# Weights loaded in pieces, blanks set by ScalarE and VectorE, smaller chunks of row maxima, and a new step order in a two-layer cross-attention and mixture-of-experts kernel

## What is computed

```python
x = x + attn0(layernorm(x), ctx, ctx)      # 16 heads of 8; 77 keys; softmax; Wo
x = x + moe0(layernorm(x))                 # 8 experts (128 -> 256 -> 128, relu squared), top 2 of 8
x = x + attn1(ctx, layernorm(x))           # 16 heads, 77 keys; relu guards; its own layernorm, gamma
x = x + block2(layernorm(x))
# block2: self-attention over 512 keys, rotary q and k, low-rank k and v;
#         r1 = rmsnorm(src + attention); shared SwiGLU + 8 routed experts (top 2 in one group);
#         rmsnorm(r1 + shared + routed)
```

## Time and profile before

| | us |
|---|---|
| median of 3 runs (range) | 365.19 (364.46 to 366.49) |
| profiled execution, its own time | 366.7 |
| its span in the trace | 364.9 |
| TensorE busy | 314.7 (86%) |
| VectorE busy | 267.6 (73%) |
| ScalarE busy | 158.9 (44%) |
| GpSimd busy | 51.4 (14%) |
| TensorE clock granted, mean | 0.944 |

### The profile page before, as it was taken

The page is one execution under the profiler, slowest core; times in us unless marked ns, Lnnn a source line. Parts: engine busy times, 40 slices in busy tenths (PEclk is TensorE's granted clock), DMA queues, the critical chain, the costliest instruction groups (busy, mean ns, idle before and its releaser), DMA issues.

```text
span 364.9 us, 5099 instructions
## 1 busy us (share of the span) xinstructions
PE 314.7 (86%) x1880; PEld 139.6 (38%) x1880; DVE 267.6 (73%) x693; ACT 158.9 (44%) x180; POOL 51.4 (14%) x40
## 2 busy tenths in 40 slices
...
GB/s 203 270 289 56 14 25 2 56 1 2 1 2 115 5 12 0 89 0 55 133 0 2 7 1 2 100 81 2 195 2 0 9 1 2 0 0 2 30 0 29
DMA packets 13448, 16.35 MB, mean 45 GB/s; under 512 B 3568, under 2 KB 12016, under 8 KB 13040
## 3 DMA queue, kind: packets, MB, share of 16 engines
...
...
## 4 chain that ended last, share of the span: by engine, by line
PE 42%; DVE 26%; issue 17%; DMA 5%; POOL 4%; ACT 3%; SPq 1%; POOLq 0%; DVEq 0%; ACTq 0%
PE pairs_ps L557 28%; DVE mx L1044 7%; PE out_ps L557 6%; PE misc_ps L557 4%; DVE mx L1048 3%; DMA qT<-qpl 3%; DMA qT<-mpl 3%; POOL pT L520 3%; DVE ACC L1214 2%; ACT pT L851 2%; DVE turned L932 1%; DVE XN L960 1%; POOL rstd L492 1%; DVE rest L932 1%; DVE ACC L932 1%
## 5 line engine op out<-in xcount | busy, mean ns | idle before, releaser
L851 ACT ACTIVATE pT<-pairs_ps 128x1024 f32<-128x1024 f32 (+1 forms) x96 | 94.4, 1022 | 84.3 <-PE pairs_ps L557 83.5
L1044 DVE TENSOR_REDUCE mx<-pairs_ps 128x2 f32<-128x1024 f32 x64 | 74.3, 1216 | 0.6 <-PE pairs_ps L557 0.3
L557 PE MATMUL pairs_ps<-experts,hid 128*128 128x128 f32 (+1 forms) x352 | 62.2, 334 | 0.1
L492 POOL TENSOR_TENSOR rstd<-var,consts 128x4 f32<-128x4 f32 x14 | 14.6, 1044 | 263.9 <-DVE var L952 134.9
L557 PEld LDWEIGHTS pairs_ps<-experts,hid 128*128 128x128 f32 x352 | 44.9, 192 | 16.0 <-issue 16.0
L557 PE MATMUL misc_ps<-ones,zeros 128*128 128x512 bf16 x138 | 43.2, 427 | 3.2 <-POOL ones L544 2.5
L557 PE MATMUL pairs_ps<-XT,experts 128*128 128x512 f32 x96 | 45.3, 614 | 0.6 <-DVE mx L1048 0.5
L557 PE MATMUL out_ps<-pT,V 128*32 128x512 f32 x256 | 33.3, 603 | 0.0
L1048 DVE TENSOR_REDUCE mx<-pairs_ps 128x8 f32<-128x616 f32 x32 | 23.7, 793 | 12.3 <-PE pairs_ps L557 12.3
L520 POOL TENSOR_SCALAR pT<-pT 77x1024 f32<-77x1024 f32 x8 | 24.9, 3126 | 38.0 <-ACT pT L851 38.0
L1214 DVE SCALAR_TENSOR_TENSOR X<-pairs_ps,gw,X 128x128 f32<-128x128 f32 x64 | 18.0, 344 | 16.0 <-PE pairs_ps L557 15.8
...
## 6 DMA issues: line engine op xcount, KB each, us to landing
qT<-qpl SPq DMA_DIRECT2D x36, 128.0 KB, 2.5
...
kT<-kpl SPq DMA_DIRECT2D x12, 128.0 KB, 2.5
...
qT<-zeros SPq DMA_DIRECT2D x6, 128.0 KB, 6.3
...
```

The source lines that it names most:

```text
L492: return pool.tensor_tensor(out, a, c, op)
L557: return nc.tensor.matmul(out, lhsT, rhs, start=start, stop=stop)
L851: nc.scalar.activation(pT[n % PT_BUFS][0:rows_, 2 * (p % 2):2 * (p % 2) + 2, :], pair_ps(step)[0:rows_, :, :], ACT.Exp, scale=SCALE[layer] ...
L1044: V_.tensor_reduce(mx[k][:, t, :, p % n], ps[:, :, :], AX.X, ALU.max).then_inc(pairs.read_sem(step), 1)
```

## The change

- Loads: `PIECES` cuts f0 and f0y into 2 transfers each and f1 into 4, by columns; readers wait for all pieces. X1 is issued before rows0. No LOAD stands ahead of the first scores but `LOAD f0 0`; rows, f0y and wb come later.
- Blanks: FILL of `qT` by SyncE (4 transfers of 128 KB) is gone. ScalarE copies zeros over both whole `qT` stacks at the start (two copies of 128 x 2048 f32), and SyncE waits for that before it stacks queries. FILL c1, c0 and k0 stand first, k1 late.
- Value tails: the memsets of the zero columns of `V` and `Vc` are gone. PV uses 9 weight columns for a head instead of 32, and one VectorE memset of `out_ps` sets the rows that are no longer written.
- Chunks of maxima: layer 0 has two chunks of 4 pairs (before one of 8), layer 1 one of 8, block2 has three, of 2, 4 and 2 pairs (before two of 4). In all 12 chunks instead of 8.
- Order: batch 0 goes ahead of batch 1. FH/FY of batch 1 come after the first scores of layer 1 (batch 0) instead of before them, and layer 1 of batch 1 is interleaved with block2's scores of batch 0.
- Filler: 194 products instead of 202.
- `SUM_ON_POOL` becomes an empty tuple and `KEYS_BY_ACT` is False: the rotations stay on VectorE and the keys' transfers on SyncE.

```diff
-CHUNK = (8, 8, 4)
+PIECES = {"wb": 1, "rows": 1, "trig": 1, "f0": 2, "f0y": 2, "f1": 4}
+CHUNKS = (((0, 4), (4, 4)), ((0, 8),), ((0, 2), (2, 4), (6, 2)))
...
+    STAT n0 0, NORM n0 0, FILL c1, FILL c0, FILL k0, STAT n0 1, CKV 0, NORM n0 1, XT n0 0, QS 0 0, LOAD f0 0, XT n0 1,
+    QS 0 1, SMAX 0 0 0 0, SMAX 0 0 1 0, SMAX 0 0 2 0, LOAD trig 0, SMAX 0 0 3 0, MCH 0 0 0, SMAX 0 0 4 0, MTR 0 0 0,
+    LOAD f0 1, SMAX 0 0 5 0, SMAX 0 0 6 0, SMAX 0 0 7 0, MCH 0 0 1, SMAX 0 1 0 0, ST 0 0 0 0, MTR 0 0 1, SMAX 0 1 1 0,
...
+    OTR 0 1 0, ST 0 1 6 0, ST 0 1 7 0, ZQ 1, RT 0, FH 0 0, FH 0 1, FH 0 2, RTE 0, FH 0 3, FY 0 0, FH 0 4, FH 0 5,
+    OC 0 1 1, ZQ 0, FY 0 1, FH 0 6, FH 0 7, FY 0 2, FY 0 3, PV 0 1 2 0, STAT n2 0, OTR 0 1 1, OC 0 1 2, OTR 0 1 2,
+    NORM n2 0, PV 0 1 3 0, OC 0 1 3, OTR 0 1 3, CKV 1, XT n2 0, XT z0 1, QS 1 0, OP 0 1, KVW, STAT n1 1, NORM n1 1,
+    SMAX 1 0 0 0, SMAX 1 0 1 0, SMAX 1 0 2 0, XT n1 1, SMAX 1 0 3 0, SMAX 1 0 4 0, SMAX 1 0 5 0, SMAX 1 0 6 0,
+    SMAX 1 0 7 0, MCH 1 0 0, FH 1 0, MTR 1 0 0, FH 1 1, RT 1, RTE 1, ST 1 0 0 0, ST 1 0 1 0, FY 1 0, ST 1 0 2 0,
...
+    Z1 0, STAT n3 0, NORM n3 0, FIN1 0, STAT n4 0, FY 1 1, FH 1 6, NORM n4 0, FY 1 2, XT n4 0, QS 2 0, FH 1 7, KP 0,
+    FY 1 3, STAT n2 1, SMAX 2 0 0 0, NORM n2 1, SMAX 2 0 0 1, SMAX 2 0 0 2, SMAX 2 0 0 3, XT n2 1, QS 1 1,
...
+    OTR 2 1 0, SMAX 2 1 7 1, ST 2 1 4 0, PV 2 1 1 2, ST 2 1 5 0, XT fl 0, SMAX 2 1 7 2, SMAX 2 1 7 3, MCH 2 1 2,
...
-FIRST_PRODUCTS = 8
+FIRST_PRODUCTS = 2
...
             def QS(step, layer, b):
-                stack(qT[b], qpl[b], Q_PART, N, after("QHI", layer, b), after("QMID", layer, b), after("QLO", layer, b),
+                sp.wait_ge(queries_blank, b + 1)
+                stack(sp, qT[b], qpl[b], Q_PART, N, after("QHI", layer, b), after("QMID", layer, b), after("QLO", layer, b),
                       q_stacked[b])
...
-                pool.memset(V[b][:, :, :, DH + 1:VW], 0.0)
...
-                    vals = V[b][:, kt, h, :] if layer == 2 else Vc[layer][b][0:rows_, h, :]
-                    last = mm(out_ps[j * VW:(j + 1) * VW, :], vals, pT[n % PT_BUFS][0:rows_, j, :],
+                    vals = V[b][:, kt, h, 0:DH + 1] if layer == 2 else Vc[layer][b][0:rows_, h, 0:DH + 1]
+                    last = mm(out_ps[j * VW:j * VW + DH + 1, :], vals, pT[n % PT_BUFS][0:rows_, j, :],
...
+                width = to.shape[1] // PIECES[name]
+                cols = slice(k * width, to.shape[1] if k == PIECES[name] - 1 else (k + 1) * width)
+                nc.scalar.dma_start(to[:, cols], src[:, cols]).then_inc(loaded[name], 16)
...
+            act.wait_ge(planes_set, 1)
+            for b in range(B):
+                blank = zeros[:, :].bitcast(F32).unsqueeze(1).broadcast_to([P, 2 * T, N // 2])
+                nc.scalar.copy(qT[b][:, :, :].bitcast(F32), blank).then_inc(queries_blank, 1)
...
-                    V_.memset(Vc[layer][b][0:C, :, DH + 1:VW], 0.0)
...
+            V_.memset(out_ps[:, :], 0.0).then_inc(blanked, 1)
```

More of the change, by code:

```diff
@@ L52 @@
 ORDER = """
[L53 to L72, removed]
@@ new lines @@
+    QS 0 1, SMAX 0 0 0 0, SMAX 0 0 1 0, SMAX 0 0 2 0, LOAD trig 0, SMAX 0 0 3 0, MCH 0 0 0, SMAX 0 0 4 0, MTR 0 0 0,
+    LOAD f0 1, SMAX 0 0 5 0, SMAX 0 0 6 0, SMAX 0 0 7 0, MCH 0 0 1, SMAX 0 1 0 0, ST 0 0 0 0, MTR 0 0 1, SMAX 0 1 1 0,
+    ST 0 0 1 0, SMAX 0 1 2 0, ST 0 0 2 0, SMAX 0 1 3 0, MCH 0 1 0, ST 0 0 3 0, PV 0 0 0 0, OC 0 0 0, ST 0 0 4 0,
+    SMAX 0 1 4 0, MTR 0 1 0, ST 0 0 5 0, PV 0 0 1 0, OC 0 0 1, ST 0 0 6 0, SMAX 0 1 5 0, OTR 0 0 0, ST 0 0 7 0,
+    PV 0 0 2 0, OC 0 0 2, OTR 0 0 1, LOAD rows 0, SMAX 0 1 6 0, SMAX 0 1 7 0, LOAD f0y 0, PV 0 0 3 0, OC 0 0 3,
```

171 lines of the change are left out of this document (91 added, 80 removed).

## The result

| | before | after |
|---|---|---|
| median of the runs, us | 365.84 (364.46 to 366.58, 4 runs) | 361.75 (359.35 to 362.36, 4 runs) |
| ratio, 95% interval | | 0.9874 (0.9836 to 0.9912) |
| profiled execution, own time, us | 366.7 | 362.36 |
| its span, us | 364.9 | 360.6 |
| mean granted clock | 0.944 | 0.945 |

A forecast was written before the change was run, and what follows sets the result against it. Limits differed by stretch: DMA first, then TensorE, VectorE without a full engine, VectorE nearly full, TensorE last. Six stretches, 19.5 + 30 + 44 + 58.6 + 123.6 + 75 = 350.7, plus 0.3, gave 351.0 us; range 341 to 361.

The forecast's parts named there:

- A: Start to first scores: 19.5 us for 26.6, with the last query transfer landing in 3.5 us.
- B: First scores to FH 0 0: 30 us for 37.5, first ST 7.3 us behind the scores, clock holding.
- the pause is some 3.5 us: TensorE's idle time before the first scores: some 3.5 us, filler and batch 1's queries keeping it going to about 16 us.
- the first rival: At the start, queries land after the full 7.4 us, TensorE pauses 7 us, the clock falls: 359 us, chance 0.13.
- E: Block2's first scores to the end of the last row-maximum reduction: 123.6 us for 97.8, VectorE receiving moved-in work.
- at the share of 0.96 instead of 0.975: VectorE's busy share from block2's scores to the last maxima: 118.7 us of work makes 123.6 us.
- The third rival: In E, late clips and normalisations stall VectorE's queue; share 0.827, 143.5 us there, 371 us in all, chance 0.07.
- The parts called free: Value tails, out_ps memset, 9-column PV weights and ScalarE's query blanks: priced at nothing, the blanks at worst 0.5 us.
- C: FH 0 0 to layer 1's first scores: 44 us for 51.4, as six FH and two FY leave it.
- D: Layer 1's first scores to block2's first scores: 58.6 us for 68.4, with 48.4 us of VectorE work.
- F: End of the last row-maximum reduction to the kernel's end: 75.0 us for 83.2, less TensorE work left.
- The second rival: Four more small chunks each expose a trip of 4.0 us instead of covering it: 367 us, chance 0.04.

The follow-up runs named there:

- experiment 2: Changed kernel with both pieces of f0 waiting until batch 1's queries have landed and trig behind the load of rows; 364.23 us, ratio 0.9981.
- experiment 3: Changed kernel with the late f0 and trig of experiment 2 and the late f1 of experiment 1; 358.99 us, ratio 0.9837.
- experiment 5: Experiment 3 plus 33 more filler products on TensorE, ahead of the first scores, MTR, ST and each score; 356.19 us, ratio 0.9780.
- experiment 10: Experiment 1 with f0 behind ST 0 0 4 0 and ST 0 0 6 0, trig behind rows, and more filler around the first scores; 355.99 us, ratio 0.9776.
- experiment 12: Experiment 10 with every load of the first 60 us placed by first use, 22 filler products ahead of first scores; 354.66 us, ratio 0.9646.
- experiment 11: Experiment 10 with the filler products of experiment 9; 355.53 us, ratio 0.9769.
- experiment 1: Changed kernel with the four pieces of f1 moved from layer 1's scores to behind four exponentials of block2's batch 0; 355.23 us, ratio 0.9746.
- experiment 6: Experiment 1 plus 28 filler products ahead of the first scores (38 instead of 10); 355.72 us, ratio 0.9764.
- experiment 8: Experiment 1 with layer 0's maxima again in one chunk of 8 pairs per batch; 366.53 us, ratio 1.0053.
- experiment 9: Experiment 6 with more filler ahead of layer 1's scores of both batches; 355.79 us, ratio 0.9742.
- experiment 7: Kernel before with only 9-column value heads, no value-tail memsets, out_ps cleared and queries blanked by ScalarE; 366.09 us, ratio 1.0059.

## Why the prediction was wrong

**A, the landing (+3.4): the step that failed is "the crowd is smaller, not gone. I take 3.5 us".** The issue of the last query transfer, the filler and ScalarE's blanks came out as worked: the two blanks took 3.70 us together and ended by 6.2 us, the last transfer went out at 15.4. But its landing was 6.79 us. The bounds were 2.3 and 7.4, and I took a value near the lower one by counting the megabytes of all of A. What counts is who is in flight in those 7 us, and I had written down myself that trig and f0's second piece would be issued at about 14 us. Experiments 2, 3, 5, 10 and 12, without them, have their first scores at 18.9 to 19.9 us and experiment 11 at 19.3; the kernel after and experiments 1, 6, 8 and 9, with them, have theirs at 22.5 to 24.3, so the crowd's price is about 4 us. No run parts f0 from trig in it.

**B, the clock (+2.7): the step that failed is "the pause is some 3.5 us", and with it that the clock then holds.** It was the first rival that came, with a pause of 6.6 us. The first ST was 9.5 us behind the scores where 7.3 were forecast, which is 2.2 of the 2.7; the rest of B was 23.1 for 22.7. Experiment 6, at clock 1.00, gives 7.6 and 30.5, so the sizes were right and the clock was not. The pause was too long because the landing was; but the step also fails by itself. In experiment 2 the landing came as forecast (19.04 us), the pause was 2.2 us, and the clock fell at 21.6. That it had held for more than 4 us of the old pause did not promise that it would hold through a shorter one with light work behind it. The rival's own sum, 359, had A nearly right (23.4 for 22.9) and took 4 us for the clock.

**E, a stop that no step of the sum contained (+5.7): the step that failed is "at the share of 0.96 instead of 0.975".** VectorE's work was forecast at 118.7 and is 116.38 us. The share was 0.90, and 5.83 us of the idle time is one wait. The third rival had a drop of that share, but from GpSimd's clips; the cause was a transfer. The error lies in the method. The prediction follows the moved LOADs only in A and has no term for a transfer in E, where the mean DMA share of 0.12 in the earlier trace rows looks harmless. The kernel after has its four LOAD f1 around QS 1 1: the rule of the prediction, that the chain's small transfers share 16 engines with the loads, held there too. The Trainium skill, "DMA: Bandwidth & Descriptors", section "Issuing engines are not separate DMA queues", is cited beside A alone. Experiment 1 takes the stop away: E 122.8 for the forecast 123.6, again by two errors that cancel, 116.1 us of work at a share of 0.945 for 118.7 at 0.96.

**Right.** C (43.7 for 44), D (58.2 for 58.6) and F (73.9 for 75.0). In C the FH and FY took 28.13 us for the forecast 28.1. Behind them the chain does not run through batch 0's norm, as worked, but through CKV 1 and SyncE's queue, which issues six context transfers ahead of the six of the queries; the norm's path had its first plane ready 0.4 us before SyncE was free, so the two are nearly equal. Three pieces of the chain of the kernel after, in C:

```profile
55.71 28.13 PE pairs_ps L564 x160
...
89.36 0.40 ACT cpl L842
...
96.80 2.42 DMA qT<-qpl
```

In D the length was right by two errors: VectorE had 45.56 us of work, not 48.4, and a share of 0.78, not 0.83. The parts called free brought nothing (experiment 7). PV of block2 went from 603 to 594 ns for one product, so four heads still run side by side. The second rival, small chunks that cost their trips, is refuted with its sign turned (experiment 8). Two slips of the working changed no verdict: E's new chunks stand in the sum at 4 us and in the account of the gains at 3.3, and the clock of before was at 0.50 until 47.2 us, not 46, so B had 4.7 us to win from it instead of 4.

**The forecast with both crowds out.** With f1 later and the start mended the kernel comes to 354.66 (experiment 12) and not to 351. C to F sum to 301.9 there and were forecast at 301.2, with no stretch off by more than 1.2 us; A and B are 1.4 us over. The other 1.6 us are none of the stretches': the forecast added 0.3 us to its span, and this profiled execution's own time is 1.9 above its span. The three shortest runs, 351.7 to 352.0, come within 1 us of 351.0. So the model of the work was good to about 2 us in 350 (D by two errors that cancel, and with more filler than the forecast had); the transfers were not in it.
